# Attention and feed-forward on one core: the order of the score tiles, maximum tiles and value product in TensorE's stream, rewritten as a pattern over four steps

## The reference, cut to what matters

```python
hid = _group_norm(xr, norm_w, norm_b)
qkv = einsum('oc,bcl->bol', qkv_w, hid) + qkv_b
weight = einsum('bhct,bhcs->bhts', q * scale, k * scale)
weight = softmax(weight, axis=-1)
a = einsum('bhts,bhcs->bhct', weight, v)
x = x + (einsum('oc,bcl->bol', proj_w, a) + proj_b)
x = x + conv1x1(gelu(rmsnorm2d(x, norm1_w)), conv_w, conv_b)
x = x + conv1x1(gelu(conv1x1(rmsnorm2d(x, norm2_w), ffn_w1, ffn_b1)), ffn_w2, ffn_b2)
```

## Time and profile before

| | |
|---|---|
| median of 3 runs | 1712.55 us (1711.57 to 1712.57) |
| the profiled execution | 1714.98 us, of which span 1713.0 us |
| granted TensorE clock, mean | 0.984 |
| TensorE matmul busy | 1675.6 us (98%) |
| VectorE busy | 1460.5 us (85%) |
| ScalarE busy | 1367.4 us (80%) |
| the chain that ended last | PE 96%, DVE 2% |

### The profile page before, as it was taken

How to read it: one execution, slowest core, us unless ns; L and a number is a source line. 1 busy time by engine, 2 the same in 40 slices (tenths; PEclk the granted TensorE clock), 3 DMA queues, 4 the chain that set the end, 5 groups by cost and what they waited for, 6 DMA issues and landing times.

```text
span 1713.0 us, 33562 instructions
## 1 busy us (share of the span) xinstructions
PE 1675.6 (98%) x12522; PEld 678.8 (40%) x12522; DVE 1460.5 (85%) x2415; ACT 1367.4 (80%) x2478; POOL 337.3 (20%) x411
## 2 busy tenths in 40 slices
PE   5999999999999999999999999999999999899999
PEld 2433333333333333333333333333333333455555
DVE  4999999999999999999999999999999995455552
ACT  2388888888888888888888888888888888666664
POOL 3101111111111111212121212121211113222220
PEclk9699999999999999999999999999999998999999
DMA  6133333333333334343333333233333320333332
GB/s 117 27 46 58 58 58 59 58 58 58 57 59 55 61 54 62 52 62 54 61 55 59 57 58 58 46 59 46 58 45 58 46 60 21 94 104 96 102 109 74
DMA packets 58625, 106.16 MB, mean 62 GB/s; under 512 B 32864, under 2 KB 33632, under 8 KB 58464
## 3 DMA queue, kind: packets, MB, share of 16 engines
q1 hardware_dynamic: 56160, 95.64, 32.7%
q10 hardware_dynamic: 2304, 8.39, 1.3%
HBM read 34.48 MB, written 9.05 MB: 25 GB/s over the span
## 4 chain that ended last, share of the span: by engine, by line
PE 96%; DVE 2%; SPq 0%; issue 0%; POOL 0%; ACT 0%; DMA 0%; DVEq 0%; POOLq 0%; ACTq 0%
PE psum L696 33%; PE psum L667 27%; PE psum L680 14%; PE psum L773 7%; PE psum L578 4%; PE psum L744 2%; PE psum L746 2%; PE psum L745 2%; PE psum L570 2%; PE psum L623 2%; DVE maxes L1022 1%; PE psum L781 1%; PE psum L591 0%; PE psum L601 0%; DVE k_high L1112 0%
## 5 line engine op out<-in xcount | busy, mean ns | idle before, releaser
L1022 DVE TENSOR_REDUCE maxes<-psum 128x1 f32<-128x512 f32 x2048 | 1276.8, 683 | 93.7 <-PE psum L667 91.7
L915 ACT ACTIVATE probs<-psum 128x512 f32<-128x512 f32 x2048 | 1110.0, 597 | 218.1 <-PE psum L680 194.5
L667 PE MATMUL psum<-k_stack,q_stack 62*128 62x512 f32 x2048 | 771.3, 456 | 1.7 <-DVE maxes L1022 0.9
L680 PE MATMUL psum<-q_stack,k_stack 64*128 64x512 f32 x2048 | 752.8, 452 | 0.0
L696 PE MATMUL psum<-probs,values 128*32 128x256 f32 (+1 forms) x7040 | 624.7, 427 | 0.7 <-ACT probs L915 0.6
L667 PEld LDWEIGHTS psum<-k_stack,q_stack 62*128 62x128 f32 x2048 | 317.0, 187 | 506.8 <-DVE maxes L1022 421.4
L680 PEld LDWEIGHTS psum<-q_stack,k_stack 64*128 64x128 f32 x2048 | 305.1, 185 | 12.3 <-issue 6.1
L696 PEld LDWEIGHTS psum<-probs,values 128*32 128x32 f32 x7040 | 138.7, 108 | 317.0 <-issue 232.6
L773 PE MATMUL psum<-probs,first_weights 128*128 128x512 f32 x256 | 116.6, 598 | 0.9 <-DVE raw L1190 0.9
L434 POOL CAST parts<-neg_max 128x16 fp32r<-128x16 f32 x64 | 12.6, 197 | 528.3 <-DVE neg_max L1001 528.3
L924 ACT ACTIVATE probs<-psum,params_sb 128x512 f32<-128x512 f32 x128 | 82.1, 686 | 20.9 <-PE psum L746 14.7
(11 more groups left out here) (95 smaller groups left out, 965.9 us busy)
## 6 DMA issues: line engine op xcount, KB each, us to landing
q_stack<-q_high SPq DMA_DIRECT2D x128, 128.0 KB, 3.9
k_stack<-k_high SPq DMA_DIRECT2D x128, 128.0 KB, 5.2
values<-inv_rms_rows SPq DMA_DIRECT2D x32, 512.0 KB, 5.0
x_sb<-in_x SPq DMA_DIRECT2D x16, 512.0 KB, 7.2
q_stack<-q_low SPq DMA_DIRECT2D x64, 128.0 KB, 6.3
k_stack<-k_low SPq DMA_DIRECT2D x64, 128.0 KB, 7.0
q_stack<-rows SPq DMA_DIRECT2D x512, 2.0 KB
attn<-raw SPq DMA_DIRECT2D x128, 64.0 KB, 2.3
```

Of the source, the lines that this page charges most:

```text
L667: nc.tensor.matmul(psum[:, BANKS + tile % BANKS, :], q_stack[used, place, p, chunk % 4, chunk // 4, :], k_stack[used, place, p, HALF * key ...
L680: nc.tensor.matmul(psum[:, tile % BANKS, :], k_stack[used, place, p, 128 * chunk:128 * chunk + 128], q_stack[used, place, p, :, t, :], sta ...
L915: nc.scalar.activation(probs[:, tile % 8, :], psum[:, tile % BANKS, :], ACT.Exp, scale=SCALE).then_inc(probs_ready, 1)
L1022: nc.vector.tensor_reduce(maxes[:, chunk // 4, j, 4 * p + chunk % 4, key_half:key_half + 1], psum[:, BANKS + max_tile(u, s, k) % BANKS, :] ...
```

## The change

`has_job` goes, and with it the two kinds of step. Instead `slot` has one order for each value of `s % 4`; `scores` gets the test for a unit that does not exist. The side job is called in every step, and does nothing where there is none. In short, with M and S tiles, the job J in its place, and V512 or V256:

- `s % 4 == 0`: S0 M0 M1 S1 S2 M2, J, V512, S3 M3
- `s % 4 == 1`: M0 S0 S1 M1, J, M2 S2 S3 M3, V512
- `s % 4 == 2`: M0 S0 S1 M1 M2 S2, J, V512, S3 M3
- `s % 4 == 3`: S0 M0 M1 S1, J, V256, M2 S2 S3 M3, V256

```diff
--- before.py
+++ after.py
@@ -640,16 +640,6 @@
                         at_least(pe, proj_taken, images_until(b - 1) * NT)
                     qk_product(c, n)
 
-            def has_job(b, half, s):
-                at = (half, s)
-                if at in (LAST_K, *VALUES):
-                    return PROLOGUE <= b + 1 < IMAGES or at == FIRST_SUMS and b == IMAGES - 1
-                if at in (GROUP_MEAN, GROUP_VAR):
-                    return has_image(b + 2)
-                if at in PROJ:
-                    return 0 < b < IMAGES
-                return half == 1 and s in QK_STEPS and PROLOGUE <= b + 2 < IMAGES
-
             def wait_for_bank(tile, freed):
 
                 at_least(pe, freed, tile - BANKS + 1)
@@ -671,6 +661,8 @@
 
             def scores(u, place, s, k):
 
+                if not has_unit(u):
+                    return
                 head, t, chunk, tile = score_head(k), s // NK, s % NK, u * TILES + 4 * s + k
                 used = slice(ROWS * (head % 2), ROWS * (head % 2) + ROWS)
                 p = head // 2
@@ -715,28 +707,63 @@
             def slot(b, parity, half, part=None):
                 u = b * 2 + half
                 for s in steps_of(part):
-
-                    broken = has_job(b, half, s)
+                    place = 2 * parity + half
                     if b == IMAGES - 1 and (half, s) == FIRST_CONV:
                         for k in range(3):
-                            scores(u, 2 * parity + half, s, k)
+                            scores(u, place, s, k)
                         weigh_before(u, parity, half, s, 0, HALF)
                         pe.wait_ge(max_taken, UNITS * TILES)
                         pe.wait_ge(weights_split, 1)
                         convolve(0, 0)
                         convolve(0, 1)
-                        scores(u, 2 * parity + half, s, 3)
+                        scores(u, place, s, 3)
                         continue
-                    middle = 2 if s % NK == 1 and not broken else 1
-                    for k in range(4):
-                        maximum_scores(u, s, k)
-                        if has_unit(u):
-                            scores(u, 2 * parity + half, s, k)
-                        if k == 1 and (broken or b < 0):
-                            side_jobs(b, parity, half, s)
-                        if k == middle and not broken:
-                            weigh_before(u, parity, half, s, 0, QUARTER)
-                    weigh_before(u, parity, half, s, 0 if broken else QUARTER, HALF)
+
+                    if s % 4 == 0:
+                        scores(u, place, s, 0)
+                        maximum_scores(u, s, 0)
+                        maximum_scores(u, s, 1)
+                        scores(u, place, s, 1)
+                        scores(u, place, s, 2)
+                        maximum_scores(u, s, 2)
+                        side_jobs(b, parity, half, s)
+                        weigh_before(u, parity, half, s, 0, HALF)
+                        scores(u, place, s, 3)
+                        maximum_scores(u, s, 3)
+                    if s % 4 == 1:
+                        maximum_scores(u, s, 0)
+                        scores(u, place, s, 0)
+                        scores(u, place, s, 1)
+                        maximum_scores(u, s, 1)
+                        side_jobs(b, parity, half, s)
+                        maximum_scores(u, s, 2)
+                        scores(u, place, s, 2)
+                        scores(u, place, s, 3)
+                        maximum_scores(u, s, 3)
+                        weigh_before(u, parity, half, s, 0, HALF)
+                    if s % 4 == 2:
+                        maximum_scores(u, s, 0)
+                        scores(u, place, s, 0)
+                        scores(u, place, s, 1)
+                        maximum_scores(u, s, 1)
+                        maximum_scores(u, s, 2)
+                        scores(u, place, s, 2)
+                        side_jobs(b, parity, half, s)
+                        weigh_before(u, parity, half, s, 0, HALF)
+                        scores(u, place, s, 3)
+                        maximum_scores(u, s, 3)
+                    if s % 4 == 3:
+                        scores(u, place, s, 0)
+                        maximum_scores(u, s, 0)
+                        maximum_scores(u, s, 1)
+                        scores(u, place, s, 1)
+                        side_jobs(b, parity, half, s)
+                        weigh_before(u, parity, half, s, 0, QUARTER)
+                        maximum_scores(u, s, 2)
+                        scores(u, place, s, 2)
+                        scores(u, place, s, 3)
+                        maximum_scores(u, s, 3)
+                        weigh_before(u, parity, half, s, QUARTER, HALF)
 
             def product(out, weights, high, low):
```

## The result

| | before | after |
|---|---|---|
| median of 4 runs | 1712.56 us (1711.57 to 1716.71) | 1701.2 us (1700.02 to 1702.68) |
| the profiled execution, span | 1713.0 us | 1700.0 us |
| TensorE matmul records, VectorE busy | 12522, 1460.5 us | 10602, 1459.1 us |

What follows compares the result with a forecast made beforehand. TensorE's order was taken to set the time, VectorE close behind through three banks. Fours summed as -88 x 0.24 - 26 x 0.35 + 10 x 0.4 = -26 us, from 1712.55 to 1686.5 us; range 1664 to 1711.

Steps and rivals of the forecast that it cites:

- unit 31: Last unit: its steps of some 2.25 us are held up by ScalarE's four exponentials (1.98) and gain at most 1 us.
- TensorE's prices: TensorE's costs: further pair 0.24 us, opening and closing a group 0.19, V256 0.57, V512 0.99, job of 512 columns 1.06.
- The rival of the dear third pair: In groups of three pairs, the third costs 0.34 us instead of 0.24: 23 us back, 1709.5 us; chance 0.09.
- The slower rival: VectorE starves behind each V512 of steps 0 and 2, idling 0.44 us instead of 0.26 and 0.11: 1746 us; chance 0.15.
- Two thirds of TensorE's gain turn into waits: Four steps with a job: TensorE alone needs 0.68 us less, but only 0.24 of it is kept.
- The layout of four steps: Timeline of four steps with a job, waits of 0.18, 0.15 and 0.11 us included: 10.59 us instead of 10.83.
- Its bank is free at 0.64: Step 0: M2 could follow at 0.58 us, but its bank is free at 0.64; ready at 0.76, 0.18 us lost.
- the 3% to spare: Steps without a job before the change: VectorE's four reductions need 2.40 us of TensorE's 2.48.
- Steps without a job: Ten fours without a job: VectorE bounds them, 10.2 to 10.35 us against 9.92, taken as 0.4 us more each.
- It is lower only where TensorE had neither value product nor jobs: TensorE's clock: stays at its upper level after the change, as it drops only without value product or jobs.
- The transfers and GpSimd: SyncE's transfers of maxima, needed five steps on, and GpSimd, which waits for VectorE: costed at nothing.
- The bounds that I worked out for the gain itself: Whole kernel: gain 19 us at 0.61 us per VectorE reduction, 28 us at 0.595.

Runs made afterwards that it cites:

- hybrid: The changed kernel with the new order only in fours that have a 512-column job in their second step, the order of before elsewhere: 1694.7 us, 0.9884.
- close_4: The changed kernel with only VectorE's final maximum moved, from step 3 (11) behind M1's reduction to step 4 (12) behind M2's: 1763.55 us, 1.0288.

## Why the prediction was right in its direction, and where it failed

The direction, the range and the mechanism held. What failed is the size: 11.4 us of 26. The steps that failed are four terms of the sum. "So the four steps take 10.59, 0.24 less than 10.83" was mis-sized, VectorE's small jobs stood in it at nothing, the "10 x 0.4" for fours without a job was too low, and unit 31 was put at no loss. Together they took back 13 us, as follows.

- **TensorE's prices** held: 0.24 us from a second to a third pair (804.19 to 804.43), 0.99 for a V512 (802.85 to 803.84), 0.57 for a V256, 1.05 for a job. The rival of the dear third pair is out, and so is the 1709.5 us that followed from it. "The trace has no group of three at full clock" was not so: step 9 of unit 29 has one, but its third tile waits for its bank, so that it has no price for the third pair. The Trainium skill (TensorE: Matmul & The Clock Gate, The mechanism) has weight loads overlap running matmuls only where the row group differs, though it names a background weight buffer as well; here third loads run under a matmul of their own row half, at 0.24 us from pair to pair, and the measurement decides.
- **The slower rival** is out too: VectorE idles 0.24 us behind the first V512 (0.26 laid out). Its 0.44 was read in the wrong place: that idle time ends at 811.25, before the V512 starts at 811.39, so it belongs to the job.
- **"Two thirds of TensorE's gain turn into waits"** was the right mechanism, and it was nearly three quarters: 0.68 of TensorE's time saved, 0.19 kept on the mean of units 2 to 28. The layout had both waits, 0.18 for VectorE and 0.26 in step 3; in place of these the runs showed 0.22 and 0.27, the second ScalarE's alone. Units 2 to 28 gained 8.8 us less than forecast, and two terms account for it (9.1 by the estimates below).
  - **The layout of four steps, mis-sized by 0.05.** "Its bank is free at 0.64. It loads its weights only then": a load that waits starts 0.05 us behind the end of the reduction (491 of the 540 maximum tiles between the 200th and the 1900th whose load starts within 0.12 us of it), and I had put this at next to nothing. The wait of M2 carries most of it, 0.04 on the path, and the V256's the rest: 10.64 instead of 10.59 in 108 fours, 5.4 us.
  - **VectorE's small jobs, left out.** Between the reductions of step 3 stands the final maximum, 0.09 us in every second four. As 41 plain fours times 0.09, this is 3.7 us; moving it away gave 3.5. In the kernel before it was covered by the 3% to spare.
- **"Steps without a job"**: the sign was right; 0.4 us each should have been 0.55, and the first four of unit 0 lost 1.15 at a lower clock, though fours in the order of before lost as much elsewhere (12.36 above), so that part may be chance. Together 2.7 us. "It is lower only where TensorE had neither value product nor jobs" did not hold in the last unit: in the kernel before the clock is 0.50 from 1430 to 1438 us, with value products running.
- **Unit 31**: "gain at most 1 us" was wrong, it lost 1.7. Four exponentials per step leave no lead, and a V512 keeps score tiles from ScalarE as it keeps maximum tiles from VectorE: in the third four ScalarE idles 1.9 us before its exponentials, where it idled 1.1 before. The hybrid took back 0.7 us there and 0.2 in the last steps; the rest lies in the four with the convolutions, 21.8 us after against 20.8 before. That four takes 20.8 to 22.1 us in the runs that have the new order in it and 19.9 to 21.5 in those that have the old one, and the cause stays open.
- **The transfers and GpSimd "at nothing"** was right for this change, but the cover was named too wide. Rows have hardly any time to spare, the projection 0.67 us, and "GpSimd waits for VectorE, not the reverse" left out TensorE, which waits for GpSimd at the projection.

These add up: -26 + 8.8 + 2.7 + 1.7, less a remainder of 0.2, give the 13 us between the profiles. That 1701.2 lies inside the range is owed to the width of the range. The bounds that I worked out for the gain itself, 19 to 28, did not hold it.

## What to carry to other kernels

When an in-order engine's saving is laid out against a neighbour that has a few per cent to spare behind few banks, every small thing that the slack used to cover comes onto the path: the 0.05 us from a release to the waiting load, and the neighbour's side jobs. List them before the sum. Follow every neighbour, too: a block that grows also delays the tile behind it, and here the next product waits for just that tile. A wait named in a view is worth a cut only if the next wait behind it is not as late: equal relief for VectorE brought 16 us in one place and nothing in another. And an order tuned for steps with a filler job should not be used where the filler is absent.

## What the runs showed that I had not expected

The kernel before showed 421 us of waits for VectorE and gained nothing in the middle from half of VectorE's maximum work. Moving 0.17 us of VectorE's work one step later cost 62 us in all, through GpSimd's queue and the clock: in `close_4` the last four of every even unit from 2 on takes 4.3 us longer on the mean, of which the wait itself is 2.45.
